# A message stage over pairs of 512 edges under one plain mask

## What is computed

```python
mid0 = w_a * xg0 * ea0
mid1 = w_b * jnp.einsum('euc,ec->eu', xg1, ea1) * INV_SQRT3
mid2 = (w_c * xg0)[:, :, None] * ea1[:, None, :]
mid3 = (w_d * ea0)[:, :, None] * xg1
mids = jnp.concatenate([mid0, mid1, mid2.reshape(-1, 3 * MUL), mid3.reshape(-1, 3 * MUL)], axis=1)
agg = jax.ops.segment_sum(mids, edge_dst, num_segments=n)
```

## Time and profile before

| | us |
|---|---|
| timed, median of three | 1999.03 |
| span of the profiled execution | 2413.3 |
| TensorE busy in the span | 1891.3 (78%) |
| VectorE busy | 1125.8 (47%) |
| ScalarE busy | 1021.4 (42%) |
| GpSimd busy | 1104.5 (46%) |
| message stage, first gather to last sum, in the profile | about 806 |

### The profile page before, as it was taken

The page is one execution under the profiler, slowest core; times in us unless marked ns, Lnnn a source line. Parts: engine busy times, 40 slices in busy tenths (PEclk is TensorE's granted clock), DMA queues, the critical chain, the costliest instruction groups (busy, mean ns, idle before and its releaser), DMA issues. The chain is left out here.

```text
span 2413.3 us, 38460 instructions
## 1 busy us (share of the span) xinstructions
PE 1891.3 (78%) x9911; PEld 1517.9 (63%) x9911; DVE 1125.8 (47%) x2791; ACT 1021.4 (42%) x3052; POOL 1104.5 (46%) x1499
## 2 busy tenths in 40 slices
PE   1368787877799858999455877787778789899699
PEld 1245454554466657999335766676767679777588
DVE  3532222222242374544664666565656669431322
ACT  2513343343353532333264555454545557454222
POOL 5547667666700004555375665565655550000243
PEclk7679999889999858999777888887888889999799
DMA  5636556565734026666544554555554553255553
GB/s 150 202 90 198 190 187 198 185 193 187 210 140 138 11 64 201 212 212 215 135 149 147 150 159 140 151 155 145 147 153 144 150 148 107 69 164 177 155 180 129
DMA packets 229197, 376.43 MB, mean 156 GB/s; under 512 B 66081, under 2 KB 114308, under 8 KB 228998
## 3 DMA queue, kind: packets, MB, share of 16 engines
q1 hardware_dynamic: 174820, 222.13, 31.0%
q0 software_dynamic: 52224, 150.15, 20.2%
q10 hardware_dynamic: 1954, 1.79, 0.2%
HBM read 275.38 MB, written 99.57 MB: 155 GB/s over the span
## 5 line engine op out<-in xcount | busy, mean ns | idle before, releaser
L1940 POOL DMA_INDIRECT msg_got<-y_dram,block_src x416 | 412.4, 991 | 293.5 <-DVE msg_prod L2012 139.7
L439 POOL DMA_INDIRECT ffn_w<-xn_dram,block_src x384 | 364.6, 949 | 219.2 <-issue 81.7
L1961 ACT ACTIVATE msg_scaled<-msg_plain,msg_w 128x125 f32<-128x125 f32 x1044 | 314.0, 386 | 280.1 <-DVE msg_plain L1993 234.6
L554 PE MATMUL sum_ps_bank<-ffn_w,sum_onehot 128*125 x928 | 270.5, 419 | 115.6 <-DVE sum_onehot L893 84.3
L554 PEld LDWEIGHTS sum_ps_bank<-ffn_w,sum_onehot 128*125 128x125 f32 x928 | 184.0, 206 | 264.6 <-issue 246.6
L881 DVE TENSOR_TENSOR agg<-sum_ps_bank,agg 125x256 f32 x232 | 98.4, 424 | 432.4 <-PE sum_ps_bank L554 216.5
L541 PE MATMUL sum_ps_bank<-sum_fc,sum_space 128*128 128x512 f32 x416 | 231.9, 644 | 68.9 <-ACT sum_space L639 48.3
L650 ACT ACTIVATE sum_space<-sum_ps_bank,sum_rec 128x128 f32<-128x128 f32 x416 | 131.0, 369 | 330.4 <-PE sum_ps_bank L541 159.5
L1982 PE MATMUL msg_ps_z<-msg_prod,msg_scaled 128*125 128x128 f32 x1416 | 207.5, 293 | 53.7 <-issue 53.0
L1982 PEld LDWEIGHTS msg_ps_z<-msg_prod,msg_scaled 128*125 128x125 f32 x1416 | 198.6, 206 | 72.4 <-issue 64.1
L2022 DVE TENSOR_TENSOR agg<-msg_ps_z,agg 125x512 f32 x232 | 159.4, 687 | 23.9 <-issue 5.2
(11 more groups left out here) (343 smaller groups left out, 3397.9 us busy)
## 6 DMA issues: line engine op xcount, KB each, us to landing
edge_w<-sum_space SPq DMA_DIRECT2D x52, 1040.0 KB
msg_w<-edge_w SPq DMA_DIRECT2D x174, 260.0 KB
ffn_run_w<-in_L_ffn_w SPq DMA_DIRECT2D x64, 512.0 KB
x_sb<-edge_w SPq DMA_DIRECT2D x58, 260.0 KB
ffn_rows<-agg SPq DMA_DIRECT2D x25, 448.0 KB
ffn_w<-in_L_ffn_w SPq DMA_DIRECT2D x16, 512.0 KB, 8.7
wd<-in_L_ffn_Wd SPq DMA_DIRECT2D x8, 1024.0 KB, 8.6
msg_got<-y_dram,block_src POOLq DMA_INDIRECT x416
```

The source lines that it names most:

```text
L439: pool.indirect_dma_start(got[:, (b + 1) % RING, u, :], None, k.x if b < RAW else k.xn_dram, bass.IndirectOffsetOnAxis(ap=k.block_src[:, b ...
L554: last = pe.matmul(ps_sum[n % ZB][0:P, :], onehot[n % OB][:, u, :], got[:, ds(need % RING, 1), u, :].rearrange("p o d -> p (o d)"), start= ...
L1940: pool.indirect_dma_start(got[:, (b + 1) % RING, u, :, :].rearrange("p k v -> p (k v)"), None, k.y_dram, bass.IndirectOffsetOnAxis(ap=k.bl ...
L1961: last = act.activation(scaled[s % MB][:, x, c, :], plain[s % MB][:, c, :], ACT.Copy, scale=w[s % RS][:, c, D + x:D + x + 1])
```

## The change

Blocks are taken two at a time in the message stage: 104 blocks of 512 edges (four chunks), 128 pairs of such a block with a tile. One plain mask is used for all 512 columns of a chunk, so a chunk is one matmul of 512 columns. The attributes, which stood in three scaled masks, go into the products:

- `along` (64 columns a chunk) is the sum over three components of y1 times attribute. ScalarE makes the first term (`first_along`), VectorE adds the second and third with scalar_tensor_tensor, in two groups of four, and multiplies by the weight at the end.
- `split`: ScalarE multiplies one product (group 8 of the buffer) by three attributes, three activations of 64 columns a chunk.
- The edge weights of a pair come in one DMA. GpSimd waits for the pair that uses a block last, from a table, once every 8 blocks of 512.
- `along_first`, `along_made`, `opened` and `split_made` are new semaphores.

```diff
-    RS, MB, ZB, XB = 4, 4, 6, 3
+    RS, MB, ZB, XB, TB, BACK = 4, 4, 6, 4, 3, 3
...
             for b in range(NB):
-                if b > AHEAD:
-                    pool.wait_ge(made, (b - AHEAD + 1) // 2)
+                if b >= 2 * RING4 and b % (2 * HOLD4) == 0:
+                    last = b // 2 - HOLD4 - 1
+                    done = pool.value_load(k.block4_done[0:1, last:last + 1], min_val=1, max_val=NP4)
+                    pool.wait_ge(made, done)
+                    pass_on(pool, freed)
...
+            def first_along(n, need):
+                act.wait_ge(w_in[n % RS], 16 * (n // RS + 1))
+                act.wait_ge(blocks_in, need)
+                if n >= TB:
+                    act.wait_ge(made, n - TB + 1)
+                for c in range(CH):
+                    last = act.activation(along[n % TB][:, c, :], got[:, ds(need % RING4, 1), c, 1, :].rearrange("p o v -> p (o v)"),
+                                          ACT.Copy, scale=w[n % RS][:, c, D:D + 1])
+                last.then_inc(along_first, 1)
+
+            def split(n):
+                act.wait_ge(opened, n + 1)
+                p = prod[n % XB]
                 for c in range(CH):
                     for x in range(3):
-                        last = act.activation(scaled[s % MB][:, x, c, :], plain[s % MB][:, c, :], ACT.Copy,
-                                              scale=w[s % RS][:, c, D + x:D + x + 1])
-                last.then_inc(scaled_made, 1)
+                        last = act.activation(p[:, c, 5 + x, :], p[:, c, 8, :], ACT.Copy, scale=w[n % RS][:, c, D + x:D + x + 1])
...
+                last.then_inc(split_made, 1)
...
+            for n in range(NP4):
+                pe.wait_ge(made, n + 1)
+                pe.wait_ge(split_made, n + 1)
+                if n >= ZB:
+                    pe.wait_ge(added, 1 + n - ZB + 1)
+                for c in range(CH):
+                    last = pe.matmul(ps_z[n % ZB][0:P, :, :], plain[n % MB][:, c, :], prod[n % XB][:, c, 0:8, :],
+                                     start=(c == 0), stop=(c == CH - 1))
                 last.then_inc(summed, 1)
...
+                dve.tensor_tensor(p[:, :, 0:9:8, :], v[:, :, 0:4:3, :], y[:, :, 0:1, :].to_broadcast([128, CH, 2, MUL]), ALU.mult)\
+                   .then_inc(opened, 1)
+                dve.wait_ge(along_first, n + 1)
+                for c in range(CH):
+                    dve.scalar_tensor_tensor(t[:, c, :], y[:, c, 2, :], w[n % RS][:, c, D + 1:D + 2], t[:, c, :], ALU.mult, ALU.add)\
+                       .then_inc(along_made, 1)
+                dve.tensor_tensor(p[:, :, 1:4, :], v[:, :, 1:2, :].to_broadcast([128, CH, 3, MUL]), y[:, :, 1:4, :], ALU.mult)
+                dve.wait_ge(along_made, 2 * CH * n + CH)
+                for c in range(CH):
+                    dve.scalar_tensor_tensor(t[:, c, :], y[:, c, 3, :], w[n % RS][:, c, D + 2:D + 3], t[:, c, :], ALU.mult, ALU.add)\
+                       .then_inc(along_made, 1)
+                if n + 1 < NP4:
+                    mask(n + 1)
+                dve.wait_ge(along_made, 2 * CH * (n + 1))
+                dve.tensor_tensor(p[:, :, 4, :], v[:, :, 2, :], t[:, :, :], ALU.mult).then_inc(made, 1)
```

Before, the statistics stood right behind the cast. TensorE gets 19 matmuls for these tables, 14 of them in fp32:

```diff
+            pe.wait_ge(four_ready, 5)
...
+            pe.wait_ge(past_made, 4)
+            pe.wait_ge(chosen_made, 4)
+            pe.wait_ge(four_ready, 6)
+            for h, (at, n) in enumerate(HALVES):
+                pe.matmul(ps_rows4[0:1, 0:NP4], even[0:n, :], past4[0:n, h, :], start=(h == 0), stop=(h == 1))
...
+            pe.wait_ge(shifted, 4)
+            pe.wait_ge(chosen_made, 6)
+            for c in range(CH):
+                for h, (at, n) in enumerate(HALVES):
+                    last = pe.matmul(ps_field4[:, c, :], dst_fb[h][0:n, :, c % KC], chosen_half[c // KC][0:n, h, :],
+                                     start=(h == 0), stop=(h == 1))
+            last.then_inc(field_ready, 1)
...
+            dve.wait_ge(tables_made, 4)
             gathered_statistics(0)
```

More of the change, by code:

```diff
@@ L218, in sum_neighbours @@
         tile_f, tile_h = early.take([EC]), early.take([EC], BF16)
+        ranks, twins, firsts = (early.take([64, 2], BF16) for x in range(3))
+        even, both, minus, first_tile = early.take([1]), early.take([2]), early.take([2], BF16), early.take([2], BF16)
+        first4, next4, offset4, even_offset, moved = (early.take([2]) for x in range(5))
+        past4, chosen4 = past[:, :, 0:NP4], chosen[:, :, 0:NP4]
+        chosen_half, tile4_row = [early.take([2, NP4]) for h in range(2)], early.take([NP4])
         low = Lent(ring[:, MARKS_AT * slot:ATTR_AT * slot])
@@ new lines, in _ @@
+            dve.tensor_copy(first_tile[:, :], tiles[:, 0, :]).then_inc(four_ready, 1)
+            dve.tensor_reduce(even[:, :], k.ident[:, 0:128:2], AX.X, ALU.add).then_inc(step, 1)
+            done[0] += 1
+            chain(dve.scalar_tensor_tensor(both[:, :], tiles[:, 0, :], -1.0, tiles[:, 1, :], ALU.add, ALU.add))
+            dve.scalar_tensor_tensor(minus[:, :], both[:, :], even[:, 0:1], tiles[:, 1, :], ALU.mult, ALU.subtract).then_inc(four_ready, 1)
+            dve.wait_ge(starts_ready, 2)
@@ new lines, in _ @@
+            chain(dve.tensor_scalar(first4[:, :], ps_four[:, 0:2], -1.0, None, ALU.mult))
+            dve.scalar_tensor_tensor(next4[:, :], ps_four[:, 2:4], -1.0, first4[:, :], ALU.mult, ALU.add).then_inc(step, 1)
+            done[0] += 1
+            chain(dve.tensor_tensor(offset4[:, :], ps_four[:, 4:6], first4[:, :], ALU.subtract))
+            dve.tensor_scalar(even_offset[:, :], offset4[:, :], even[:, 0:1], None, ALU.mult).then_inc(four_ready, 1)
+            for h in range(2):
+                dve.tensor_scalar(past4[:, h, :], k.iota[:, 0:NP4], next4[:, h:h + 1], None, ALU.is_ge).then_inc(past_made, 1)
@@ new lines, in _ @@
+            chain(dve.tensor_tensor(moved[:, :], offset[:, :], offset4[:, :], ALU.subtract))
+            for h in range(2):
+                dve.wait_ge(past_made, h + 3)
+                dve.scalar_tensor_tensor(chosen4[:, h, :], k.iota[:, 0:NP4], first4[:, h:h + 1], past4[:, h, :], ALU.is_ge, ALU.subtract)\
+                   .then_inc(chosen_made, 1)
+            chain(dve.tensor_scalar(moved[:, :], moved[:, :], float(P), None, ALU.mult))
+            for h, (at, n) in enumerate(HALVES):
+                dve.tensor_scalar(dst_fb[h][0:n, :, :], dst_fb[h][0:n, :, :], moved[0:n, h:h + 1], None, ALU.add).then_inc(shifted, 1)
@@ new lines, in _ @@
+            dve.tensor_scalar(k.pair4_tile[0:1, :], tile4_row[0:1, :], float(T - 1), None, ALU.min).then_inc(tables_made, 1)
+            done[0] += 1
+            dve.tensor_copy(k.block4_done[0:1, :], ps_rows4[0:1, 256:256 + NB:2]).then_inc(tables_made, 1)
+            dve.wait_ge(field_ready, 2)
+            dve.scalar_tensor_tensor(k.pair4_dst[:, :, :].rearrange("p n c -> p c n"),
+                                     k.iota[:, 0:NP4].unsqueeze(1).to_broadcast([128, CH, NP4]), float(-P),
+                                     ps_field4[:, :, :], ALU.mult, ALU.add).then_inc(tables_made, 1)
@@ L1898, in sum_messages @@
         ps_lanes, lanes_made, rest_zero = ph.ps("lanes", [128, P]), ph.sem("lanes_made"), ph.sem("rest_zero")
-        w_in, got_in, blocks_in = ph.sems("w_in", RS), ph.sems("got_in", RING), ph.sem("blocks_in")
-        rest, rested = ph.sb("rest", [128, 32]), ph.sem("rested")
-        masked, scaled_made, made, summed, added = (
-            ph.sem(x) for x in ("masked", "scaled_made", "made", "summed", "added"))
+        w_in, got_in, blocks_in = ph.sems("w_in", RS), ph.sems("got_in", 2 * RING4), ph.sem("blocks_in")
+        rest, rested, freed = ph.sb("rest", [128, 32]), ph.sem("rested"), ph.sem("freed")
+        masked, opened, along_first, along_made, split_made, made, summed, added = (
+            ph.sem(x) for x in ("masked", "opened", "along_first", "along_made", "split_made", "made", "summed", "added"))
         block = ph.ctx.enter_context(nc.Block())
@@ L2028, in _ @@
             mask(0)
[L2029 to L2046 removed]
+            need = place(0)
+            for n in range(NP4 + BACK):
+                if n < NP4:
+                    products(n, need)
+                if n >= BACK:
+                    tile = dve.value_load(k.pair4_tile[0:1, n - BACK:n - BACK + 1], min_val=0, max_val=T - 1)
+                if n + 1 < NP4:
+                    need = place(n + 1)
+                if n >= BACK:
+                    add_sum(n - BACK, tile)
+                if n == NP4 - 1:
                     dve.wait_ge(raw_in, 128)
```

192 lines of the change are left out of this document (91 added, 101 removed).

## The result

The changed kernel takes 2128.58 us (median of 4 runs, 2124.02 to 2134.07) against 1996.16 for the kernel before (4 runs): a ratio of 1.0658 with a 95% interval of 1.0634 to 1.0683. It is slower, as forecast, but by 132 us in place of 61, and lies above the range, which ended at 2110. Of all the runs in this document one stands apart, the third of experiment 7 at 3682.98 us; the time and the ratio given there leave it out.

What follows compares the result with a forecast made beforehand. VectorE was taken to bound the changed message stage (128 x 4.6 + 15 = 604 us), VectorE and GpSimd level before (555). Stage +49, tables +12: 1999 + 61 = 2060 us, range 1990 to 2110.

Steps and rivals of the forecast that it cites:

- The stalls of the profile before: Message stage before: the profile's 806 us include stalls that timed runs cannot have; timed stage taken as 555 us.
- The upper bound of 590: Timed message stage before: at most 590 us, if the rest of the program has little to give.
- TensorE's 61 us: Message stage: TensorE's matmuls take 442 us, 61 less than before, worth nothing since TensorE does not end last.
- VectorE's pair: Message stage: a pair costs VectorE 4.6 us, between 3.95 and 5.3, the wait for `along_made` covered; 589 us for 128.
- The small operations' price: VectorE's eight scalar_tensor_tensor of 64 columns a pair: 0.20 us each, 1.60 together, bounds 0.12 and 0.28 each.
- GpSimd hidden behind VectorE: Message stage: the same 416 gathers, 2.59 us a block, 539 us, hidden behind VectorE's 589.
- ScalarE beside VectorE: Message stage: sixteen activations take ScalarE 3.8 us a pair, at most 4.6, beside VectorE's 4.6.
- Tables: New tables ahead of the first gathered statistics: +12 us, between 8 and 16, all charged to the time.
- rival 1: Message stage: stall partly real, 668 us when timed; it goes and the stage ends at 604: 1947 us; chance 0.13.
- rival 2: Message stage: small operations near 0.12 us, GpSimd sets the end on both sides: 2011 or 1999 us; chance 0.13.
- Rival 3: Message stage: small operations cost 0.28 us each, a pair 5.3: 2149 us with the tables; chance 0.11.
- rival 4: Message stage: TensorE falls to 1.2 GHz, a pair takes 6.9 us, the stage 883; chance 0.03.

Runs made afterwards that it cites:

- experiment 7: Kernel before with VectorE's order changed to three products, a sum, three products, the mask, a sum: 2027.49 us, ratio 1.0160.
- experiment 1: The kernel before, unchanged, profiled again: 1991.84 us, span 1990.1.
- experiment 5: Kernel before with eight of TensorE's 32 matmuls of a step left out: 1993.71 us against 1994.45, ratio 0.9993.
- experiment 2: Changed kernel with VectorE's two register loads moved ahead of the wait for `along_made`: 2072.65 us, ratio 1.0389.
- experiment 13: On experiment 2, the two large products take their second operand from PSUM, gathered features left out: 2044.18 us, ratio 1.0246.
- experiment 4: Kernel before with only the new tables added, unused by its message stage: 2007.38 us against 1993.62, ratio 1.0067.
- experiment 3: On experiment 2, one wide product of 512 columns and two adds replace the eight small operations: 2069.93 us.
- experiment 6: Kernel before with VectorE's mask put between the two sums of a step: 2022.54 us, ratio 1.0149.
- experiment 12: On experiment 2, the eight small operations multiply by constants in place of attributes: 2087.75 us, ratio 1.0464.
- experiment 9: On experiment 2, the running sum `along` lies in PSUM, not SBUF: 2068.66 us, ratio 1.0363.
- experiment 11: On experiment 9, the eight small operations multiply by constants in place of attributes: 2028.16 us, ratio 1.0169.
- experiment 8: Changed kernel with one wide product and two adds for the eight small operations, loads ahead of the last product: 2054.57 us, ratio 1.0302.
- experiment 10: On experiment 8, the running sum `along` lies in PSUM, not SBUF: 2053.38 us, ratio 1.0284.

## Why the forecast missed

- **The stalls of the profile before.** Right: experiment 1 has a stage of 559.7 us where 555 was worked out, and VectorE's step at 4.58 in mid-stage. (The upper bound of 590 beside it follows from no row; the sum did not use it.)
- **TensorE's 61 us.** Right that they are worth nothing (experiment 5).
- **VectorE's pair.** This is the step that failed. The prediction says: "The order puts a product between the two groups of four and a mask behind the second, which cover the wait for `along_made`." They cover it for the engine, not for what stands behind the waiting product. The product's wait lasts until the second group ends (1505.28), and until then the two register loads, 0.62 us each, don't run; 1.24 us of loads against 0.59 + 0.33 us of mask and product. By rows the uncovered rest is 0.55, and the product shows its whole 0.42 in place of 0.33: 0.64 x 128 = 82 us, of which 5 are given back by the other terms (4.56 in place of 4.6): 77, and the stage missed by 76. All the other terms were right: 0.60, 0.78, 0.87, 0.78, 0.59 and 0.61, and with the loads moved the pair is 4.56 against a forecast of 4.6 (experiment 2). The prediction priced the loads nowhere; in the kernel before they ran under products that waited for nothing (experiment 1: the four loads of a step from 1496.43 to 1499.06, the six products from 1496.69 to 1499.32).
- **The small operations' price.** Right, 0.196 against 0.20. The prediction set the Trainium skill's price for operations on SBUF against the earlier trace rows, which read PSUM: not like with like. What those rows and the new operations share is a scalar read for each partition, and the price hangs on that (last section).
- **GpSimd hidden behind VectorE.** Right in the changed kernel, where the gap lets GpSimd wait. It would have been the next miss: at 4.56 us a pair a block takes 2.96 us in place of the 2.59 taken from the earlier trace rows, and the stage 628.7 in place of 604. Experiment 13 shows that the large products do this; without it the stage is 599.4. ScalarE beside VectorE was right too, 4.02 us a pair against 3.8.
- **Tables.** Right: 11.4 us later at the stage's start, 9 to 17 in the timed runs (experiment 4), forecast 12.
- **The sum.** 1996 + 120 + 11 = 2127; measured 2128.58. The miss of 69 us (2128.58 - 2060) is the 76 of the stage's 680 in place of 604, less the 5 us by which the stage before was longer than taken and the 3 by which the median before is lower with its fourth run. In experiment 13, which is free of the gap and of most long gathers (and leaves the gathered features out of two products), 48 us are left against the forecast's 61.
- **The rivals.** 1 falls with experiment 1, 2 with the pair of 5.20 us. Rival 3's pair of 5.3 us is close in number but not in cause: the small operations start 0.196 us apart, as in the earlier trace rows. 4 falls: the granted clock in the stage is 0.98.

The Trainium skill (Perfetto Trace Analysis, DVE / Act Engine Instruction (TENSOR_ADD, Activation, etc)) says that the sequencer goes on to the next instruction once the waiting one is in a hardware wait queue. For register loads the traces disagree: in the changed kernel the load begins 0.05 us after the operation that the product waits for has ended, in experiment 3 the same 0.05 us after the add, and both times it had nothing of its own to wait for. A queue that is full does not explain it: in experiment 2 the first load begins at 1517.43 ahead of five operations that had been given out before it and have not begun, in experiment 3 it stands behind three at most.

## What to carry over

In these traces register loads on VectorE (0.62 us each) that stood behind a waiting instruction waited too: count them, and put them ahead of the wait. A wait that lies in the shadow of other work is free only if nothing behind it has a price of its own. Before a second engine is written down as hidden, ask what its pace becomes once the first one runs without gaps.

## What the runs showed of the hardware

- A gather that begins while VectorE multiplies two tensors in SBUF is let go when that operation ends, and takes 0.82 us more (1671 of 1681 long gathers); some are let go only by a later operation of the row, after up to 2.76 us in all in experiment 6 and 2.86 in 12. The Trainium skill has this as a rule (SBUF — State Buffer, Who interferes with whom): a VectorE instruction with two SBUF inputs contends with a GpSimd instruction that reads SBUF, and what they share is an exclusive lock. Experiment 13 agrees: 57 long gathers in place of 224. (A gather reads its row numbers, `block_src`, from SBUF.)
- A faster VectorE can make the kernel slower for that reason: 4.57 to 4.33 us a step, and 28 to 33 us more (experiments 6 and 7); 4.56 to 4.07 us a pair, and 15 us more (experiment 12 against 2). I know the mechanism from the rows, but have no rule that says beforehand how the two engines will fall against each other.
- A scalar_tensor_tensor of 64 columns starts every 0.196 us with its scalar read from SBUF for each partition (experiment 2; 0.192 with the addend in PSUM, experiment 9), every 0.135 with a constant (experiment 12; 0.131 with the addend in PSUM, experiment 11). The Trainium skill's price that the prediction weighed (0.13 us, an estimate from Perfetto Trace Analysis, Optimizing Scalar/DVE Operations) is met by the second form, not by the first.
- No version here beats the kernel before. Of the changed design's versions that leave nothing out, experiments 8 and 10 are the fastest, 3.0 and 2.8% slower than the kernel before.
